# Router logits computed with the tokens as the stationary operand, straight into token rows

## The chip, the cores and the metric

One Trainium2 chip, one of its cores. The metric is the device time of one launch in microseconds (us), lower is better. The kernel before takes 298.62 us, the median of 3 runs (298.42 to 298.67). Its engines are named as the profile names them: PE is TensorE's matmul side, PEld the loading of its stationary operand, ACT is ScalarE, DVE is VectorE, POOL is GpSimd, SP is SyncE.

## The reference

One transformer block over `x` of 8 sequences of 256 tokens, 256 wide: layer norm with adaptive scale and shift, a two-pass attention, a second layer norm, and a mixture of 8 experts with 2 chosen for each token, beside a shared feed-forward part. What the change touches is the router:

```python
h = hidden_states.reshape(-1, H)                                   # 2048 tokens x 256
logits = h.astype(jnp.float32) @ gate_weight.astype(jnp.float32).T # 2048 x 8
scores = jax.nn.softmax(logits, axis=-1)
topk_w, topk_i = _group_limited_topk(scores)
...
g = jnp.einsum('th,nfh->ntf', h, gate_w)
u = jnp.einsum('th,nfh->ntf', h, up_w)
e = jnp.einsum('ntf,nhf->nth', jax.nn.silu(g) * u, down_w)
routed = jnp.einsum('nth,tn->th', e, wmat)
shared = jax.nn.silu(h @ sh_gate_w.T) * (h @ sh_up_w.T) @ sh_down_w.T
```

## The kernel before

There are three stretches. Until about 142 us of the profile, attention of the 8 sequences `b` is interleaved with the router and the shared feed-forward part of earlier sequences; until about 200 us the rest of the shared part (`pe_up(q, j)`, `pe_down(q)`) runs; then 39 tiles of 128 routed rows go through their experts. Every engine works through a list written out by hand (from line 1502 on), in its own order; engines meet only through semaphores, which are waited for with `wait_ge`. An instruction that waits holds up everything behind it on its engine.

A product in full precision is made of three matmuls (`mm3`, line 341): each operand is kept as a rounded part `_hi` and a remainder `_lo`, and lo x hi, hi x lo and hi x hi are added in PSUM. The first operand of `mm3` is the stationary one, which is loaded into the array; the second one is streamed through it.

The router runs in pairs of sequences `p` (512 tokens, 4 blocks of 128). For each sequence `b`: `dve_h2` makes the normalised rows, `pe_h2t` transposes them into a PSUM bank (`post_bank(b)`, bank `HB[1]` except for `b` = 7), `act_h2` copies the rounded part into `h2T_hi`, and `dve_h2_lo` subtracts to get `h2T_lo` (semaphore `h2_lo`). `pe_logits(b)` then takes the 8 columns of router weights `wrt` as stationary operand and streams 256 tokens, for 2 halves `k` of the width: 6 matmuls, and a result of 8 rows x 256 tokens. `act_lg(b)` copies it to SBUF (`lg`), and `pe_logits_t(p)` transposes the four blocks of a pair into token rows, 128 x 8 each, in `LOG` (columns 0 to 31 of `HB[1]`). `dve_select(p, 0)` waits for these (`lt_done`), and two rounds of top-1 follow; then `pe_rank(p)` counts the slots of each expert, `dve_slots` and 8 indirect DMAs of POOL (`pool_scatter`) write the rows to DRAM.

Four orders matter for the steps below. Behind `pe_logits(0)` on PE stands `pe_v(4)` (line 1066), which waits for ACT to have emptied its banks (`act_qk(5, 0)`). Behind `pe_logits(2)` stands `pe_pt(5, True)` (line 1109), which waits for the exponentials of sequence 5 (`act_exp`, line 1137). Behind `pe_logits(3)` stand `pe_s1(7)` and `pe_up(1, 1)`, which waits for a product of DVE (`dve_gate(1, 0)`, line 457). Behind `pe_logits(4)` stands `pe_up(2, 0)`, which waits for `dve_og(1)` (line 471).

Of the kernel before, what the change touches and what calls it, by code (L numbers as in the profile page):

```python
# [28 lines left out]
def adaln_block(nc, x_in, w_qkv, b_cols, w_proj, b_proj, gate_col, cam_w0, cam_w1,  # L29
# [17 lines left out]
    with ExitStack() as ctx:  # L47
        def sb(name, shape, dt=F32):
            return ctx.enter_context(nc.sbuf_tensor(name, shape, dt))
# [4 lines left out]
        def sem(name):  # L54
            return ctx.enter_context(nc.semaphore(name))
# [57 lines left out]
        s_ident_ready = sem("ident_ready")  # L113
        s_lg_copied = sem("lg_copied")
        s_lg_done = sem("lg_done")
        s_lt_done = sem("lt_done")
# [157 lines left out]

        lg = [sb(f"lg{u}", [NE, S]) for u in range(2)]
        sact = [sb(f"sact{u}", [P, S]) for u in range(2)]
# [61 lines left out]
        def parts(t, *idx):  # L338
            return t[0][idx], t[1][idx]
# [190 lines left out]
        def pe_h2t(pe, b):  # L530
            pe.wait_ge(s_h2_ready, b + 1)
            if b == B - 1:
                pe.wait_ge(s_og_ready, 3)
            elif b % 2:
                pe.wait_ge(s_lg_copied, b)
            elif b >= 2:
                pe.wait_ge(s_slots_ready, b // 2)
            for d in range(KD):
                for t in range(TT):
                    last = pe.transpose(post_bank(b)[:, d * S + t * P:d * S + (t + 1) * P],  # L540
                                        h2all[:, b % 4 * TT + t, d * P:(d + 1) * P], ident[:])
            last.then_inc(s_h2t_done, 1)

        def pe_logits(pe, b):
            pe.wait_ge(s_wlo_later, 1)
            pe.wait_ge(s_h2_lo, b + 1)
            for k in range(KD):
                last = mm3(pe, post_bank(b)[0:NE, 0:S], parts(wrt, slice(None), k),
                           parts(h2T, slice(None), k, ring4(b)), k == 0, k == KD - 1)
            last.then_inc(s_lg_done, 1)  # L550

# [6 lines left out]
        def dve_h2_lo(dve, b):  # L558
            dve.wait_ge(s_h2_hi, b + 1)
            dve.tensor_tensor(h2T[1][:, :, ring4(b)], bank(post_bank(b)), h2T[0][:, :, ring4(b)].bitcast(F32),  # L560
                              ALU.subtract).then_inc(s_h2_lo, 1)

        def act_lg(act, b):
            act.wait_ge(s_lg_done, b + 1)
            if b >= 2:
                act.wait_ge(s_lt_done, b // 2)
            act.activation(lg[b % 2][:], post_bank(b)[0:NE, 0:S], ACT.Copy).then_inc(s_lg_copied, 1)


        def pe_logits_t(pe, p):  # L570
            pe.wait_ge(s_lg_copied, 2 * p + 2)
            for j in range(NB):
                last = pe.transpose(LOG[:, j * NE:(j + 1) * NE], lg[j // TT][:, j % TT * P:(j % TT + 1) * P], ident[0:NE, 0:NE])
            last.then_inc(s_lt_done, 1)

# [182 lines left out]
        if True:  # L758
# [742 lines left out]
            with nc.Block() as block:  # L1501
# [149 lines left out]
                def _(act):  # L1651
# [66 lines left out]
                    act_qk(act, 5, 0)  # L1718
                    act_lg(act, 0)
                    act_norm(act, 4)  # L1720
# [8 lines left out]
                    act_norm(act, 5)  # L1729
                    act_lg(act, 1)  # L1730
                    act_exp(act, 4, True)
# [16 lines left out]
                    act_qk(act, 7, 1)  # L1748
                    act_lg(act, 2)
                    act_pt(act, 5, True)  # L1750
# [5 lines left out]
                    act_weights(act, 4)  # L1756
                    act_lg(act, 3)
                    act_exp(act, 7, False)
# [18 lines left out]
                    act_gate(act, 2, 0)  # L1777
                    act_lg(act, 4)
                    act_h2(act, 5)
                    act_hi(act, 2, 0)  # L1780
                    act_gate(act, 2, 1)
                    act_lg(act, 5)
                    act_hi(act, 2, 1)
# [13 lines left out]
                    act_h2(act, 7)  # L1797
                    act_lg(act, 6)
                    act_hi(act, 3, 2)
                    act_lg(act, 7)  # L1800
                    act_route(act, 3)
# [236 lines left out]
                def _(pe):  # L2038
# [55 lines left out]
                    pe_up(pe, 0, 0)  # L2094
                    pe_logits(pe, 0)
                    pe_v(pe, 4)
# [7 lines left out]
                    pe_s2_cam(pe, 4)  # L2104
                    pe_logits(pe, 1)
                    pe_up(pe, 0, 1)
                    pe_pt(pe, 5, False)
                    pe_logits_t(pe, 0)
                    pe_qk(pe, 6)
# [10 lines left out]
                    pe_out(pe, 4)  # L2120
                    pe_logits(pe, 2)
                    pe_pt(pe, 5, True)
# [4 lines left out]
                    pe_pt(pe, 6, False)  # L2127
                    pe_logits(pe, 3)
                    pe_s1(pe, 7)
                    pe_up(pe, 1, 1)  # L2130
                    pe_logits_t(pe, 1)
                    pe_v(pe, 6)
# [14 lines left out]
                    pe_pt(pe, 7, True)  # L2147
                    pe_logits(pe, 4)
                    pe_up(pe, 2, 0)
                    pe_out(pe, 7)  # L2150
                    pe_h2t(pe, 5)
                    pe_up(pe, 2, 1)
                    pe_logits(pe, 5)
                    pe_logits_t(pe, 2)
                    pe_up(pe, 2, 2)
# [9 lines left out]
                    pe_h2t(pe, 7)  # L2165
                    pe_logits(pe, 6)
                    pe_logits(pe, 7)
                    pe_logits_t(pe, 3)
                    pe_down(pe, 3)
# [81 lines left out]
```

## Time and profile before

| what | value |
|---|---|
| median of the runs | 298.62 us |
| the profiled execution's own time | 299.12 us |
| its span (first to last instruction) | 297.3 us |
| PE busy, PEld busy | 259.9 us (87%), 240.3 us (81%) |
| DVE, ACT, POOL busy | 190.1, 161.2, 128.4 us |
| chain that ended last, by engine | PE 77%, DVE 5%, ACT 4%, issue 4% |

The span is the part that the trace covers; 1.8 us of the profiled execution's own time lie around it. The chain that ended last is followed back from the last instruction: a change of PE's time counts where PE stands in it. A line number is one of the kernel before.

### The profile page before, as it was taken

How to read it: one execution, taken by the hardware profiler on the slowest of the kernel's cores; microseconds unless marked ns; L12 is line 12 of the kernel's file. 1: busy time of each engine (PE TensorE's matmuls, PEld its weight loads, DVE VectorE, ACT ScalarE, POOL GpSimd, SP SyncE). 2: the span in 40 equal slices, each digit the busy share in tenths (PEclk: the TensorE clock that was granted, in tenths of full speed). 3: DMA queues.
4: the chain of work that ended last, by engine and by line, in shares of the span. 5: the costliest groups of instructions: out<-in, count | busy, mean ns of one | idle time of the engine just before them, and what ended most of it. 6: DMA issues, size and time to landing. Idle time of an engine off the chain costs nothing.

```text
span 297.3 us, 6191 instructions
## 1 busy us (share of the span) xinstructions
PE 259.9 (87%) x1820; PEld 240.3 (81%) x1820; DVE 190.1 (64%) x579; ACT 161.2 (54%) x429; POOL 128.4 (43%) x146
## 2 busy tenths in 40 slices
PE   1799999899999999999997691999999999999900
PEld 1697698778988999979896581999999999999800
DVE  2667765259987754864897552365546566858894
ACT  2538477877558548474374621345656565555500
POOL 3120406454460287769927572001545444544540
PEclk9999999999999999999999996799999999999975
DMA  7893033450242022321501243043444365584454
GB/s 237 279 341 77 0 84 137 117 171 32 77 110 73 1 92 89 110 89 54 165 0 57 90 163 127 4 125 107 128 142 127 128 210 179 179 245 149 150 193 139
DMA packets 29319, 36.98 MB, mean 124 GB/s; under 512 B 4468, under 2 KB 23903, under 8 KB 29288
## 3 DMA queue, kind: packets, MB, share of 16 engines
q1 hardware_dynamic: 24056, 27.19, 30.7%
q0 software_dynamic: 3408, 8.46, 7.6%
q10 hardware_dynamic: 1824, 0.94, 1.1%
q8 instruction: 16, 0.26, 0.4%
q14 instruction: 15, 0.12, 0.1%
HBM read 24.78 MB, written 12.71 MB: 126 GB/s over the span
## 4 chain that ended last, share of the span: by engine, by line
PE 77%; DVE 5%; ACT 4%; issue 4%; another core or an unknown queue 2%; DMA 2%; POOL 2%; ACTq 1%; POOLq 0%; DVEq 0%
PE bank L343 18%; PE bank L345 17%; PE bank L344 17%; PE bank L1133 3%; PE bank L1370 3%; PE bank L1348 3%; PE bank L1105 2%; PE bank L1125 2%; PE bank L1088 2%; PE bank L1116 2%; PE bank L1097 2%; PE bank L1006 1%; DMA mh<-routed_out 1%; DMA routed_out<-yo_all,dest 1%
## 5 line engine op out<-in xcount | busy, mean ns | idle before, releaser
L1436 POOL DMA_INDIRECT routed_out<-yo_all,dest x39 | 40.1, 1028 | 65.1 <-ACT yo_all L1397 49.2
L343 PE MATMUL bank<-experts_w,h2T_lo 128*128 (+1 forms) x156 | 50.7, 325 | 0.0
L345 PE MATMUL bank<-experts_w,h2T_hi 128*128 (+1 forms) x156 | 47.2, 303 | 0.0
L344 PE MATMUL bank<-experts_w,h2T_hi 128*128 (+1 forms) x156 | 47.0, 301 | 0.0
L701 POOL DMA_INDIRECT routed_in<-h2all,slot_u x32 | 31.6, 988 | 21.2 <-DVE slot_u L687 13.3
L1425 DVE SCALAR_TENSOR_TENSOR wstage<-wstage,wt,bank 128x176 f32<-128x176 f32 x39 | 15.5, 397 | 28.8 <-ACT wstage L1387 28.8
L343 PEld LDWEIGHTS bank<-experts_w,h2T_lo 128*128 128x128 f32 (+1 forms) x156 | 29.6, 190 | 0.5 <-issue 0.5
L344 PEld LDWEIGHTS bank<-experts_w,h2T_hi 128*128 128x128 f32 (+1 forms) x156 | 29.7, 190 | 0.0
L343 PE MATMUL bank<-h2T_hi,wsgu_lo 128*128 128x256 f32 (+1 forms) x96 | 28.3, 295 | 1.5 <-issue 1.5
L345 PEld LDWEIGHTS bank<-experts_w,h2T_hi 128*128 128x128 f32 (+1 forms) x156 | 29.4, 188 | 0.0
L345 PE MATMUL bank<-h2T_hi,wsgu_hi 128*128 128x256 f32 (+1 forms) x96 | 27.4, 285 | 0.5 <-issue 0.5
L344 PE MATMUL bank<-h2T_lo,wsgu_hi 128*128 128x256 f32 (+1 forms) x96 | 27.3, 284 | 0.5 <-issue 0.5
L1387 ACT ACTIVATE wstage<-bank 128x176 f32<-128x176 f32 x39 | 12.4, 317 | 22.2 <-PE bank L345 22.2
L343 PE MATMUL bank<-hT_hi,wqk_lo 128*128 128x256 f32 x64 | 20.2, 316 | 2.0 <-DVE hT_lo L1218 2.0
L1397 ACT ACTIVATE yo_all<-bank 128x256 f32<-128x256 f32 x39 | 15.0, 385 | 11.8 <-PE bank L345 7.5
L343 PE MATMUL bank<-wsd_hi,aT_lo 128*128 128x256 f32 (+1 forms) x48 | 15.0, 313 | 6.5 <-DVE aT_lo L463 6.5
L343 PEld LDWEIGHTS bank<-h2T_hi,wsgu_lo 128*128 128x128 f32 (+1 forms) x96 | 17.6, 184 | 2.0 <-issue 1.7
L344 PE MATMUL bank<-hT_lo,wqk_hi 128*128 128x256 f32 x64 | 19.0, 298 | 0.0
L1142 ACT ACTIVATE exchange<-bank,nm 128x256 f32<-128x256 f32 x32 | 14.8, 472 | 7.8 <-DVE nm L1203 6.1
L345 PE MATMUL bank<-hT_hi,wqk_hi 128*128 128x256 f32 x64 | 19.0, 297 | 0.0
L345 PEld LDWEIGHTS bank<-h2T_hi,wsgu_hi 128*128 128x128 f32 (+1 forms) x96 | 17.6, 184 | 1.2 <-issue 1.2
L344 PEld LDWEIGHTS bank<-h2T_lo,wsgu_hi 128*128 128x128 f32 (+1 forms) x96 | 17.6, 184 | 0.1
(248 smaller groups left out, 761.2 us busy)
## 6 DMA issues: line engine op xcount, KB each, us to landing
h2all<-routed_in SPq DMA_DIRECT2D x39, 130.0 KB, 2.1
wstage<-gu_t SPq DMA_DIRECT2D x8, 352.0 KB
res<-x SPq DMA_DIRECT2D x4, 512.0 KB, 8.9
mx<-modrow SPq DMA_DIRECT2D x8, 256.0 KB, 3.8
mh<-modrow SPq DMA_DIRECT2D x8, 256.0 KB
exchange<-routed_out SPq DMA_DIRECT2D x8, 256.0 KB
wmod_s<-w_mod SPq DMA_DIRECT2D x3, 512.0 KB, 9.7
wstage<-down_t SPq DMA_DIRECT2D x8, 176.0 KB
```

Source lines behind the costliest of these rows:

```text
L343: pe.matmul(out_ap, l[1], r[0], start=start, stop=False)
L344: pe.matmul(out_ap, l[0], r[1], start=False, stop=False)
L345: return pe.matmul(out_ap, l[0], r[0], start=False, stop=stop)
L701: pool.indirect_dma_start(out=routed_in, out_offset=bass.IndirectOffsetOnAxis(slot_u[:, i, j:j + 1], 0), in_=h2all[:, j % (2 * NB), :], in ...
L1133: last = pe.matmul(TR[u][:, t * D:(t + 1) * D], PT[u][:, k, t * P:(t + 1) * P], VV[u][:, k, P:P + D], start=(k == 0), stop=(k == TT - 1))
L1142: last = act.activation(pr[u][:, t, :], Sb[u][:, t * S:(t + 1) * S], ACT.Exp, bias=nm[u][:, i, t:t + 1], accum_out=ls[u][:, i, t:t + 1])
L1348: last = pe.transpose(XTb[r % 2][:, d * P:(d + 1) * P], xt_in[t % 8][:, d * P:(d + 1) * P], ident[:])
L1370: last = pe.transpose(ATb[r % 2][0:FH, j * P:(j + 1) * P], av[r % 2][:, j * FH:(j + 1) * FH], ident[:])
L1387: act.activation(sg[r % 2], EGU[r % 2][:, 0:F], ACT.Silu).then_inc(s_esilu, 1)
L1397: act.activation(yo[t % 6], EDN[r % 2][:, 0:D], ACT.Copy).then_inc(s_ey_ready, 1)
L1425: dve.scalar_tensor_tensor(av[q], sg[q], wt[:, t % 8:t % 8 + 1], EGU[q][:, F:2 * F], ALU.mult, ALU.mult).then_inc(s_ea_ready, 1)
L1436: pool.indirect_dma_start(out=routed_out, out_offset=bass.IndirectOffsetOnAxis(dest[:, t % 16:t % 16 + 1], 0), in_=yo[t % 6], in_offset=No ...
```

## The change

`pe_logits` now works on a pair: for each of its four blocks of 128 tokens and each half of the width, the 128 columns of `h2T` are the stationary operand and the 8 columns of `wrt` are streamed, so that the result lands in `LOG` as token rows. The ACT copies `act_lg`, the buffers `lg`, the transposes `pe_logits_t` and two semaphores go. The new group stands where `pe_logits_t(p)` stood in PE's list, and waits for the remainders of both sequences (`h2_lo` of 2p + 2); `pe_h2t` of an odd sequence waits for `h2_lo` of the sequence before it in place of the copy.

```diff
@@ pe_h2t
             elif b % 2:
-                pe.wait_ge(s_lg_copied, b)
+                pe.wait_ge(s_h2_lo, b)
...
-        def pe_logits(pe, b):
+        def pe_logits(pe, p):
             pe.wait_ge(s_wlo_later, 1)
-            pe.wait_ge(s_h2_lo, b + 1)
-            for k in range(KD):
-                last = mm3(pe, post_bank(b)[0:NE, 0:S], parts(wrt, slice(None), k),
-                           parts(h2T, slice(None), k, ring4(b)), k == 0, k == KD - 1)
-            last.then_inc(s_lg_done, 1)
+            pe.wait_ge(s_h2_lo, 2 * p + 2)
+            for b, u in pair_of(p):
+                for t in range(TT):
+                    j = u * TT + t
+                    at = slice(b % 4 * S + t * P, b % 4 * S + (t + 1) * P)
+                    for k in range(KD):
+                        last = mm3(pe, LOG[:, j * NE:(j + 1) * NE], parts(h2T, slice(None), k, at),
+                                   parts(wrt, slice(None), k), k == 0, k == KD - 1)
+            last.then_inc(s_lt_done, 1)
...
-        def act_lg(act, b):
-            act.wait_ge(s_lg_done, b + 1)
-            if b >= 2:
-                act.wait_ge(s_lt_done, b // 2)
-            act.activation(lg[b % 2][:], post_bank(b)[0:NE, 0:S], ACT.Copy).then_inc(s_lg_copied, 1)
-
-        def pe_logits_t(pe, p):
-            pe.wait_ge(s_lg_copied, 2 * p + 2)
-            for j in range(NB):
-                last = pe.transpose(LOG[:, j * NE:(j + 1) * NE], lg[j // TT][:, j % TT * P:(j % TT + 1) * P], ident[0:NE, 0:NE])
-            last.then_inc(s_lt_done, 1)
...
-                    act_lg(act, 0)
...
                     pe_up(pe, 0, 0)
-                    pe_logits(pe, 0)
                     pe_v(pe, 4)
...
                     pe_s2_cam(pe, 4)
-                    pe_logits(pe, 1)
                     pe_up(pe, 0, 1)
                     pe_pt(pe, 5, False)
-                    pe_logits_t(pe, 0)
+                    pe_logits(pe, 0)
                     pe_qk(pe, 6)
...
                     pe_h2t(pe, 7)
-                    pe_logits(pe, 6)
-                    pe_logits(pe, 7)
-                    pe_logits_t(pe, 3)
+                    pe_logits(pe, 3)
                     pe_down(pe, 3)
```

On PE, between the shared part of sequence 0 and the values of sequence 4, the kernel before had these instructions (`wrt` are the router weights, `wv` the value weights; the first shape is that of the result):

```order
L345 MATMUL bank3<-h2T_hi,wsgu_hi 128x256
L343 MATMUL bank3<-h2T_hi,wrt_lo 8x256 [waits h2_lo,wlo_later]
L344 MATMUL bank3<-h2T_lo,wrt_hi 8x256
L345 MATMUL bank3<-h2T_hi,wrt_hi 8x256
L343 MATMUL bank3<-h2T_hi,wrt_lo 8x256
L344 MATMUL bank3<-h2T_lo,wrt_hi 8x256
L345 MATMUL bank3<-h2T_hi,wrt_hi 8x256
L343 MATMUL bank2<-wv_hi,hT0_lo 128x384 [waits kl,qk_second,qk_first,wlo]
```

They are gone from there: `pe_v(4)` now follows the shared part at once, with the same waits.

On PE, at the end of the router of the last pair, ahead of `pe_down(3)` (`lg` is the ACT copy, `wsd` the shared down weights), the kernel before had:

```order
L344 MATMUL bank3<-h2T_lo,wrt_hi 8x256
L345 MATMUL bank3<-h2T_hi,wrt_hi 8x256
L573 MATMUL bank3<-ident,lg0 128x8 [waits lg_copied]
L573 MATMUL bank3<-ident,lg0 128x8
L573 MATMUL bank3<-ident,lg1 128x8 x2
L343 MATMUL bank0<-wsd_hi,aT1_lo 128x256 [waits wlo_later,a_lo_dve]
```

and the kernel after the change has there (the first of 8 such threes, and what stands ahead of them):

```order
L537 MATMUL bank3<-ident,h2all 128x128 [waits og_ready,h2_ready]
L537 MATMUL bank3<-ident,h2all 128x128 x3
L340 MATMUL bank3<-wrt_hi,h2T_lo 128x8 [waits h2_lo,wlo_later]
L341 MATMUL bank3<-wrt_lo,h2T_hi 128x8
L342 MATMUL bank3<-wrt_hi,h2T_hi 128x8
```

Two groups of 6 matmuls with a result of 8 x 256 and four transposes have become one group of 24 matmuls with a result of 128 x 8, and its only waits stand at its head.

## Rows read from the trace of the kernel before

**Rows 1.** The page, parts 1 and 4: busy time, and the chain's shares.
```profile
PE 259.9 (87%) x1820; PEld 240.3 (81%) x1820; DVE 190.1 (64%) x579; ACT 161.2 (54%) x429; POOL 128.4 (43%) x146
...
PE 77%; DVE 5%; ACT 4%; issue 4%; another core or an unknown queue 2%; DMA 2%; POOL 2%; ACTq 1%; POOLq 0%; DVEq 0%
```

**Rows 2.** Groups of instructions: busy us, mean ns of one | idle before, releaser.
```profile
L343 PE MATMUL bank<-h2T_hi,wrt_lo 128*8 128x256 f32 x16 | 4.9, 307 | 1.2 <-DVE h2T_lo L560 1.1
...
L343 PEld LDWEIGHTS bank<-h2T_hi,wrt_lo 128*8 128x8 f32 x16 | 1.4, 87 | 2.1 <-issue 1.7
...
L343 PEld LDWEIGHTS bank<-h2T_hi,wsgu_lo 128*128 128x128 f32 x64 | 12.1, 189 | 1.9 <-issue 1.7
...
L567 ACT ACTIVATE lg<-bank 8x256 f32<-8x256 f32 x8 | 2.9, 363 | 1.7 <-PE bank L345 1.0 <-issue 0.6
```

**Rows 3.** Timeline, PE: start us, us, engine, line, stationary*shape, streamed shape [idle before].
```profile
6.40 3.56 PE L998 MATMUL bank<-cS,wmod_s 128*128 128x8 f32 x16 [6.40 <-DVE cS L909]
...
15.18 0.41 PE L345 MATMUL bank<-hT_hi,wqk_hi 128*128 128x256 f32 x1
15.39 0.41 PE L343 MATMUL bank<-hT_hi,wqk_lo 128*128 128x256 f32 x1
...
100.47 0.29 PE L597 MATMUL bank<-r_sel,ones 128*128 128x24 bf16 x6
```

**Rows 4.** Timeline, PE and (last row) ACT, 80 to 96 us: pair 0.
```profile
80.28 0.28 PE L343 MATMUL bank<-h2T_hi,wsgu_lo 128*128 128x256 f32 x1
...
81.70 0.28 PE L343 MATMUL bank<-h2T_hi,wrt_lo 128*8 128x256 f32 x1
...
83.11 0.41 PE L343 MATMUL bank<-wv_hi,hT_lo 128*128 128x384 f32 x1 [0.55 <-issue]
...
94.79 0.41 PE L573 MATMUL bank<-ident,lg 8*128 8x8 f32 x4
95.13 0.39 PE L343 MATMUL bank<-hT_hi,wqk_lo 128*128 128x256 f32 x1
...
82.54 0.48 ACT L1183 ACTIVATE KT<-bank,cols 128x256 f32<-128x256 f32 x1
```

**Rows 5.** Timeline, PE, ACT and DVE, 108 to 129 us: pair 1.
```profile
109.13 0.60 PE L1116 MATMUL bank<-ident,exchange 128*128 128x128 f32 x4
...
117.99 0.39 PE L343 MATMUL bank<-h2T_hi,wsgu_lo 128*128 128x256 f32 x1
...
119.62 0.41 PE L573 MATMUL bank<-ident,lg 8*128 8x8 f32 x4
...
128.43 0.66 PE L1116 MATMUL bank<-ident,exchange 128*128 128x128 f32 x4 [0.54 <-ACT exchange L1150]
...
108.45 0.20 ACT L1142 ACTIVATION_READ_ACCUMULATOR exchange<-bank,nm 128x1 f32 x1
...
117.52 0.42 DVE L457 TENSOR_TENSOR aact<-aact,bank 128x256 f32<-128x256 f32 x1
```

**Rows 6.** Timeline, DVE and PE, 137 to 146 us: pair 2.
```profile
137.41 0.69 DVE L471 TENSOR_TENSOR og<-bank,gring 128x512 f32<-128x512 f32 x1 [2.41 <-issue]
...
142.77 0.69 DVE L560 TENSOR_TENSOR h2T_lo<-bank,h2T_hi 128x512 fp32r<-128x512 f32 x1 [0.19 <-ACT h2T_hi L556]
...
138.34 0.28 PE L343 MATMUL bank<-h2T_hi,wsgu_lo 128*128 128x256 f32 x1
...
145.27 0.36 PE L343 MATMUL bank<-h2T_hi,wsgu_lo 128*96 128x256 f32 x1
```

**Rows 7.** Timeline, DVE and PE, 159 to 163 us: pair 3.
```profile
159.03 1.46 DVE L560 TENSOR_TENSOR h2T_lo<-bank,h2T_hi 128x512 fp32r<-128x512 f32 x2 [0.72 <-ACT h2T_hi L556]
...
162.30 0.39 PE L343 MATMUL bank<-wsd_hi,aT_lo 128*128 128x256 f32 x1
```

**Rows 8.** Windows (stretch, length, PE busy, granted clock), and longest waits.
```profile
184.50:190.20 5.70, 5.70 (x26) 0.50 0.07 23
...
ACT sact L435 <- remote: 7.0, 1, 7.0
```

More of the change, by code:

```diff
@@ L113, in adaln_block @@
         s_ident_ready = sem("ident_ready")
-        s_lg_copied = sem("lg_copied")
-        s_lg_done = sem("lg_done")
         s_lt_done = sem("lt_done")
@@ L272, in adaln_block @@
         slot_u = sb("slot_u", [P, 2, NR], U32)
-        lg = [sb(f"lg{u}", [NE, S]) for u in range(2)]
         sact = [sb(f"sact{u}", [P, S]) for u in range(2)]
@@ L1729, in _ @@
                     act_norm(act, 5)
-                    act_lg(act, 1)
                     act_exp(act, 4, True)
@@ L1748, in _ @@
                     act_qk(act, 7, 1)
-                    act_lg(act, 2)
                     act_pt(act, 5, True)
@@ L1756, in _ @@
                     act_weights(act, 4)
-                    act_lg(act, 3)
                     act_exp(act, 7, False)
@@ L1777, in _ @@
                     act_gate(act, 2, 0)
-                    act_lg(act, 4)
                     act_h2(act, 5)
@@ L1781, in _ @@
                     act_gate(act, 2, 1)
-                    act_lg(act, 5)
                     act_hi(act, 2, 1)
@@ L1797, in _ @@
                     act_h2(act, 7)
-                    act_lg(act, 6)
                     act_hi(act, 3, 2)
-                    act_lg(act, 7)
                     act_route(act, 3)
@@ L2120, in _ @@
                     pe_out(pe, 4)
-                    pe_logits(pe, 2)
                     pe_pt(pe, 5, True)
@@ L2127, in _ @@
                     pe_pt(pe, 6, False)
-                    pe_logits(pe, 3)
                     pe_s1(pe, 7)
                     pe_up(pe, 1, 1)
-                    pe_logits_t(pe, 1)
+                    pe_logits(pe, 1)
                     pe_v(pe, 6)
@@ L2147, in _ @@
                     pe_pt(pe, 7, True)
-                    pe_logits(pe, 4)
                     pe_up(pe, 2, 0)
@@ L2152, in _ @@
                     pe_up(pe, 2, 1)
-                    pe_logits(pe, 5)
-                    pe_logits_t(pe, 2)
+                    pe_logits(pe, 2)
                     pe_up(pe, 2, 2)
```

## The prediction

> **What bounds the kernel now.** I read the page's busy times and the shares of the chain first: PE is busy 87% of the span and holds 77% of the chain that ended last [rows 1]. So time added to PE counts, unless PE was going to wait there anyway, and time taken from ACT (54%) counts only where PE waits for it. Then the groups of instructions: the router's product is 48 matmuls, three groups like the one shown, with 8 stationary and 256 streamed columns; the copies are 8, of 363 ns [rows 2]. Then the timeline around each of the four pairs, for what PE waits for there [rows 4 to 7].
>
> **The pace of a matmul.** Durations of PE are latencies that overlap, so the cost is the distance between starts. With 128 stationary and 256 streamed columns it is (81.70 - 80.28) / 12 = 0.118 us [rows 4]; loading only 8 stationary columns makes it no faster, since the 256 streamed ones set it. After the change 128 columns are loaded and 8 streamed, and the load has to set the pace. A load of 8 columns takes 87 ns and one of 128 takes 189 ns [rows 2]: 102 ns for 120 more columns. The one place with this very shape is L998: 16 in 3.56 us, and with the last one's 0.36 taken off, 3.20 / 15 = 0.213 between starts [rows 3]. The clock was at its lower level there: the 256-column matmuls after it start 0.21 apart [rows 3], as they do (5.70 / 26 = 0.219) where the granted clock is 0.50 [rows 8]. At the full clock half of 0.213 is 0.107.
>
> Ends for the new shape: from below 0.048, the bf16 matmuls of the rank (0.29 / 6 [rows 3]), or 0.085, the four transposes with 128 loaded and 8 streamed columns ((95.13 - 94.79) / 4 [rows 4]); from above 0.189, a whole load with nothing beside it. Since loads of this kind already fit under a pace of 0.118, I take the middle of 0.107 and 0.118, 0.112. A pair's 24 matmuls then take 2.69 us. Before, it had 12 x 0.118 = 1.42 for the products and 0.34 for the transposes. So PE gets 0.93 us more work a pair; where PE waited, the old work was partly free, and I go pair by pair.
>
> The Trainium skill (TensorE: Matmul & The Clock Gate, section LDWEIGHTS) prices a load by its columns, at 1.2 GHz: 128 of them make 107 ns, which the halved pace of L998 bears out. The same page, section on what overlaps in packed matmuls, says that a load runs beside a matmul only in another row group; by that each of the 24 would pay the load in full, 0.189, and the sum below would be 11.9 us instead of 4.5. The trace disagrees: loads of 189 ns stand under a pace of 0.118.
>
> **Pair 0.** Taking `pe_logits(0)` (6 x 0.118 = 0.71) from its place gains nothing: `pe_v(4)` behind it starts at 83.11 because ACT empties its bank until 82.54 + 0.48 = 83.02 [rows 4]. Taking `pe_logits(1)` gains 0.70; the transposes and the wait for the copy ahead of them 0.43 (0.34, and 0.09 above the normal distance). Net +2.69 - 1.13 = +1.56.
>
> **Pair 1.** `pe_logits(2)` hid a wait: the transposes behind it, at 109.13, need exponentials that end at 108.65, so they move up by 0.43 at most [rows 5]. `pe_logits(3)` gains nothing: `pe_up(1, 1)` at 117.99 follows the product that DVE ends at 117.94 [rows 5], whatever PE does before. Transposes and wait: 0.44. Net +2.69 - 0.87 = +1.82. Then comes the cover: PE sat idle 0.54 ahead of 128.43 for ACT's normalised scores [rows 5], and being late fills that gap, -0.54. That holds although the selection starts later on DVE, with the scores' reciprocal queued behind it: DVE starts it about 2.9 us later, has some 0.9 of idle time to give back, and is then still ahead of PE. Net +1.28.
>
> **Pair 2.** Taking `pe_logits(4)` moves `pe_up(2, 0)` from 138.34 only to the end of DVE's product at 138.10: -0.2 with the semaphore [rows 6]. The new group needs `h2_lo` of both, which DVE ends at 143.46; 0.05 for the semaphore and 2.69 end it at 146.20, where the next group began at 145.27 [rows 6]: +0.93. Net +0.73. Here ACT's copies did stand in the path, and their going is in this number.
>
> **Pair 3.** Both remainders are ready at 159.03 + 1.46 = 160.49 [rows 7]. Before, PE began on sequence 6 at 159.87, ahead of that; the added wait costs this head start. 160.54 + 2.69 = 163.23 against 162.30 [rows 7]: +0.93. Behind the waiting matmul stand `pe_down(3)`, the rank and the order; ACT's `act_shared(3)`, the slots, the scatters and the tables wait for these, so all of it moves by the same.
>
> ACT loses 8 x 0.36 = 2.9 us [rows 2]; beyond the places named, it lies beside PE and gives nothing. DMAs and queues are not touched. From 164 us on the work is the same and hangs on PE's order, so I cost it at nothing.
>
> **Sum.** 1.56 + 1.28 + 0.73 + 0.93 = 4.50 us on 299.12, 303.6; on the median, which lies 0.5 lower, 303.1. In general it is 96 times the pace less 6.26 us. At 0.107 the time is 302.6, at 0.118 303.7; at 0.085 300.5; at 0.189 310.5. Zero is at 0.065.
>
> **Rival 1, the load costs little (not slower).** If the array takes the next 128 columns in the background as fast as it does for the bf16 rank, the streamed columns set the pace and 8 are almost none. At 0.048 the group of 24 takes 1.15 and the pairs give +0.02, 0, -0.81 and -0.61: -1.4, 297.2. With the latency of one taken off, the rank's pace is 0.024, and the same sum is about -3.5, 295.1. It decides below 0.065. For it: rank and transposes load 128 columns at that pace [rows 3, 4]. Against: these are bf16 or transposes, and loads of the router's kind take 102 ns more for 120 more columns.
>
> The Trainium skill (same page, Back-to-back issue gap) has a rule for this rival: a warm matmul of 1 to 64 streamed columns costs about 60 cycles, an estimate of 0.6 us for a group of 24. Its section on loads speaks against it; L998 sides with the loads.
>
> **Rival 2, the clock falls.** For 2.7 us PE would stream almost nothing, four times, in pair 3 right after an idle stretch. After L998's 3.56 us of the same shape the clock was still at the lower level [rows 3]. A fall cost, the one time it is seen, 26 starts in 5.70 us instead of 26 x 0.118 = 3.07: 2.6 us [rows 8]. One fall gives 305.7, two 308.3, four 313.5. Against it: the clock stayed up through 160 us with several waits of PE of 1 to 2 us, and L998 began on an idle engine, so it doesn't tell whether this shape would hold a clock that is up.
>
> **Rival 3, the long wait at 176 us changes.** ACT waits 7.0 us for a matmul group's semaphore that the trace ascribes to no engine [rows 8]; PE then stands idle and restarts at the lower clock, 6.5 + 2.6 = 9.1 us together. If PE's shifted schedule dissolves it, the time is 294.0; it could also grow by some us. Against: scatters, their semaphores and PE's order all shift alike.
>
> **How the numbers follow.** Forecast (300.5 to 304.5) 0.46; rival 2 0.30; rival 1 0.12; rival 3 0.12, of which 0.07 shorter. The predicted time is 303.1. A measurement of this kernel can tell about 0.2% (0.6 us) from no change. Faster: 0.11 of rival 1 and 0.07 of rival 3, 0.18. Within: 0.04, from paces near 0.065. Slower 0.78. The range goes from 297.0 (half of rival 1 inside) to 310.5 (three falls of the clock, or loads without any overlap); about 0.13 is left below and 0.07 above.
>
> **What would show it.** The starts of the 24 matmuls: 2.6 to 2.8 us a group says the load sets the pace, 0.6 to 1.2 says rival 1. The granted clock in and after the groups tells rival 2. `pe_v(4)` should still begin right after ACT's KT; `pe_up(1, 1)` right after DVE's product; PE's idle time ahead of the scores of sequence 7 should be gone; PE's copy waits ahead of the transposes too. The expert stretch should have its old length, and the long wait of ACT should be there again, some 4.5 us later. Wrong would be a shift of the last router group's end by less than 3 us, or idle time of PE that is new.

## The result, and the profile after

The changed kernel takes 309.32 us (median of 4 runs, 308.26 to 310.76) against 298.52 for the kernel before beside it: 1.0364 of it, 95% interval 1.0329 to 1.0399. It is 10.8 us slower, where 4.5 were forecast, and the time lies inside the range given, at its upper end. The profiled execution took 308.83 us, its span is 307.1, and the mean granted clock 0.935 against 0.963. First the busy times and the chain's shares (page, parts 1 and 4), which answer to [rows 1]:

```profile
PE 271.4 (88%) x1852; PEld 253.8 (83%) x1852; DVE 190.3 (62%) x579; ACT 158.4 (52%) x421; POOL 128.2 (42%) x146
...
PE 78%; ACT 6%; DVE 5%; issue 4%; DMA 2%; another core or an unknown queue 2%; ACTq 1%; POOLq 0%; POOL 0%; DVEq 0%
```

PE is busy 11.5 us longer with 32 instructions more. The timeline of PE shows the group of pair 0 and the product behind it, which answers to [rows 4] (start us, us, engine, line, operands):

```profile
93.08 0.25 PE L340 MATMUL bank<-wrt_hi,h2T_lo 128*128 128x8 f32 x1
...
95.65 0.25 PE L342 MATMUL bank<-wrt_hi,h2T_hi 128*128 128x8 f32 x1
95.77 0.36 PE L340 MATMUL bank<-hT_hi,wqk_lo 128*128 128x256 f32 x1
...
96.40 0.41 PE L341 MATMUL bank<-hT_lo,wqk_hi 128*128 128x256 f32 x1
...
99.39 0.39 PE L340 MATMUL bank<-hT_hi,wqk_lo 128*128 128x256 f32 x1
```

The 24 matmuls take 95.77 - 93.08 = 2.69 us, 0.112 each: the pace assumed. But behind them the matmuls of 256 columns start (99.39 - 96.40) / 14 = 0.214 us apart, where the kernel before has 0.118. The windows say why (stretch, length, then busy us of each engine, granted clock, DMA share, GB/s); they answer to [rows 8]:

```profile
92.00:96.20 4.20, 4.20 (x39) 4.20 (x38) 1.44 (x5) 2.19 (x8) 0.00 (x0) 1.00 0.19 48
96.20:99.60 3.40, 3.40 (x18) 3.40 (x17) 2.84 (x14) 1.25 (x3) 0.00 (x0) 0.50 0.00 0
...
123.50:126.90 3.40, 3.40 (x13) 3.40 (x13) 2.46 (x12) 0.00 (x0) 2.85 (x4) 0.50 0.58 159
...
150.80:154.20 3.40, 3.40 (x18) 3.40 (x18) 1.25 (x10) 0.38 (x1) 2.96 (x4) 0.50 0.23 80
...
167.90:181.50 13.60, 12.80 (x76) 12.41 (x77) 6.03 (x27) 5.28 (x11) 5.94 (x7) 0.50 0.17 59
...
195.20:198.60 3.40, 3.22 (x15) 3.22 (x16) 0.45 (x2) 0.00 (x0) 0.00 (x0) 0.50 0.12 39
```

The clock is at 0.50, 1.2 GHz, four times behind or in a router group, and once more behind the idle stretch at the end. The first fall comes after 4.2 us in which PE shows no idle time at all; for 2.7 of them it had streamed 8 columns a matmul. The expert stretch is as long as before: from the first to the last matmul that reads expert weights (the last two times of each row, first of the kernel before, then of the change; tile experts_w) it is 82.4 and 82.3 us.

```profile
L343 PE MATMUL bank<-experts_w,h2T_lo x156: 277/323/408, 199.8 to 282.2; 128*128 x78, 88*128 x78
L340 PE MATMUL bank<-experts_w,h2T_lo x156: 277/323/407, 209.6 to 291.9; 128*128 x78, 88*128 x78
```

Three rows answer to [rows 4, 5]: ACT's KT and `pe_v(4)`, then DVE's product, `pe_up(1, 1)` and the scores of sequence 7.

```profile
81.68 0.48 ACT L1171 ACTIVATE KT<-bank,cols 128x256 f32<-128x256 f32 x1
82.26 0.41 PE L340 MATMUL bank<-wv_hi,hT_lo 128*128 128x384 f32 x1 [1.25 <-ACT KT L1171]
...
119.14 0.42 DVE L454 TENSOR_TENSOR aact<-aact,bank 128x256 f32<-128x256 f32 x1
119.61 0.39 PE L340 MATMUL bank<-h2T_hi,wsgu_lo 128*128 128x256 f32 x1
...
133.08 0.60 PE L1104 MATMUL bank<-ident,exchange 128*128 128x128 f32 x4
```

Both waits stand where they were forecast, right behind ACT's KT and DVE's product, and the idle time ahead of the scores is gone. Pairs 2 and 3 (timeline, DVE and PE) answer to [rows 6, 7]:

```profile
147.26 0.69 DVE L561 TENSOR_TENSOR h2T_lo<-bank,h2T_hi 128x512 fp32r<-128x512 f32 x1 [0.19 <-ACT h2T_hi L557]
150.77 0.48 PE L340 MATMUL bank<-h2T_hi,wsgu_lo 128*96 128x256 f32 x1
...
166.05 1.46 DVE L561 TENSOR_TENSOR h2T_lo<-bank,h2T_hi 128x512 fp32r<-128x512 f32 x2 [0.72 <-ACT h2T_hi L557]
167.65 0.24 PE L340 MATMUL bank<-wrt_hi,h2T_lo 128*128 128x8 f32 x1 [1.83 <-DVE h2T_lo L561]
172.56 0.56 PE L340 MATMUL bank<-wsd_hi,aT_lo 128*128 128x256 f32 x1
...
195.38 0.58 PE L340 MATMUL bank<-wsd_hi,aT_lo 128*128 128x256 f32 x1 [4.23 <-DVE aT_lo L460]
```

Pair 2: 2.8 us from the end of DVE's remainder to the next group, as forecast. Pair 3: PE waits for both remainders, and the clock falls just after the group has begun, so that it takes 172.56 - 167.65 = 4.9 us, not 2.7. Against [rows 4 to 7] the kernel is late by 0.64 at 95.77, 4.65 at 133.08, 5.50 at 150.77 and 10.26 at 172.56; at 195.38 it is 10.88 [rows 8], and the whole profiled execution 9.71. It had been 13.1 late at 190.62, ahead of PE's idle stretch, where the kernel before was at 177.50. ACT's long wait is there again, but 5.5 us in place of 7.0, PE's idle stretch 4.2 in place of 6.5, and the half clock at the end of it lasts 3.4 us with 3.2 of work in place of 5.7 [rows 8]. At the first expert matmul the kernel is 9.8 late (209.6 against 199.8). So 3.3 us (13.1 to 9.8) of what was lost came back there:

```profile
ACT sact L432 <- remote: 5.5, 1, 5.5
```

### The profile page after: what moved, and what is told of

It reads as the page before. It is cut to its first block, busy times and chain, and to the rows that moved or that the text cites. A ratio compares the mean times of both kernels' runs of the same rounds, so it can differ in the third digit from the quotient of the medians.

```text
span 307.1 us, 6237 instructions
## 1 busy us (share of the span) xinstructions
PE 271.4 (88%) x1852; PEld 253.8 (83%) x1852; DVE 190.3 (62%) x579; ACT 158.4 (52%) x421; POOL 128.2 (42%) x146
## 4 chain that ended last, share of the span: by engine, by line
PE 78%; ACT 6%; DVE 5%; issue 4%; DMA 2%; another core or an unknown queue 2%; ACTq 1%; POOLq 0%; POOL 0%; DVEq 0%
PE bank L340 19%; PE bank L342 18%; PE bank L341 18%; PE bank L1358 3%; PE bank L1336 3%; PE bank L1076 2%; PE bank L1113 2%; PE bank L1121 2%; PE bank L1085 2%; PE bank L1093 2%; PE bank L1104 2%; DMA mh<-routed_out 1%; PE bank L994 1%; DMA routed_out<-yo_all,dest 1%
## 5 line engine op out<-in xcount | busy, mean ns | idle before, releaser
L340 PE MATMUL bank<-h2T_hi,wsgu_lo 128*128 128x256 f32 (+1 forms) x96 | 29.8, 311 | 2.5 <-issue 1.4
L341 PE MATMUL bank<-h2T_lo,wsgu_hi 128*128 128x256 f32 (+1 forms) x96 | 28.3, 295 | 0.0
L342 PE MATMUL bank<-h2T_hi,wsgu_hi 128*128 128x256 f32 (+1 forms) x96 | 28.2, 294 | 0.0
L340 PEld LDWEIGHTS bank<-h2T_hi,wsgu_lo 128*128 128x128 f32 (+1 forms) x96 | 18.6, 194 | 3.1 <-ACT og L474 1.1
L341 PEld LDWEIGHTS bank<-h2T_lo,wsgu_hi 128*128 128x128 f32 (+1 forms) x96 | 18.7, 195 | 0.6 <-issue 0.6
L342 PEld LDWEIGHTS bank<-h2T_hi,wsgu_hi 128*128 128x128 f32 (+1 forms) x96 | 18.6, 194 | 0.0
```

Source lines behind the costliest of these rows:

```text
L340: pe.matmul(out_ap, l[1], r[0], start=start, stop=False)
L341: pe.matmul(out_ap, l[0], r[1], start=False, stop=False)
L342: return pe.matmul(out_ap, l[0], r[0], start=False, stop=stop)
```

## The experiments

One thing has to be known to read the times: the kernel before took 298.5 and 299.3 us on two of the chips and 287.9, 288.1 and 288.5 on three others. On the latter ACT's long wait, PE's idle stretch behind it and its half clock are all missing (below). So each run is set against the kernel before on its own chip, and the clean account is made where that wait is missing.

| kernel | us | before | ratio (95%) |
|---|---|---|---|
| e1 wide streams | 304.87 | 299.28 | 1.0176 (1.0104 to 1.0249) |
| e2 old form, new places | 302.39 | 299.28 | 1.0123 (1.0055 to 1.0191) |
| e3 pair 0 only | 300.18 | 299.28 | 1.0056 (1.0019 to 1.0093) |
| e4 mixed | 316.52 | 299.28 | 1.0589 (1.0522 to 1.0656) |
| e5 filler | 293.41 | 287.85 | 1.0197 (1.0166 to 1.0228) |
| e6 only pair 3 wide | 297.11 | 287.85 | 1.0328 (1.0287 to 1.0369) |
| e7 pair 3 only | 292.46 | 287.85 | 1.0169 (1.0128 to 1.0210) |
| e8 late pads | 299.19 | 287.85 | 1.0415 (1.0365 to 1.0466) |
| e9 the change again | 299.30 | 288.06 | 1.0421 (1.0358 to 1.0484) |
| e10 wide streams again | 291.39 | 288.06 | 1.0136 (1.0086 to 1.0186) |
| e12 pair 0 only, again | 290.30 | 288.06 | 1.0088 (1.0058 to 1.0119) |
| e13 fewer loads, wide | 290.07 | 288.46 | 1.0056 (1.0039 to 1.0073) |
| e14 fewer loads, narrow | 291.75 | 288.46 | 1.0097 (1.0070 to 1.0124) |
| e15 old form, new places, again | 292.65 | 288.46 | 1.0138 (1.0118 to 1.0158) |
| e16 filler again | 293.27 | 288.46 | 1.0164 (1.0141 to 1.0187) |

**Is it the few streamed columns?** e1 and e10 stream 256 columns:

```diff
-                        last = mm3(pe, LOG[:, j * NE:(j + 1) * NE], parts(h2T, slice(None), k, at),
-                                   parts(wrt, slice(None), k), k == 0, k == KD - 1)
+                        last = mm3(pe, HB[1][:, j * NE:j * NE + 32 * NE].rearrange("p (r e) -> p r e", e=NE),
+                                   parts(h2T, slice(None), k, at),
+                                   [wrt[i][:, k:k + 1, :].to_broadcast([P, 32, NE]) for i in range(2)],
+                                   k == 0, k == KD - 1)
```

> The new form with one difference: each of the 96 matmuls streams 256 columns (the 8 router columns repeated 32 times) in place of 8; same 128 loaded columns, same places, same waits. Theory (the clock falls because these groups stream almost nothing): no half-clock stretch at the four groups, pace 0.118 a matmul, group of 24 in 2.8 us, time 303.2 to 304.6 us although 31 times as many columns are streamed. Rival 1 (it is the loads, or the places and waits, that lose the time): the surplus stays and the wider streams add 96 x 0.006 = 0.6, 309.9 us. Rival 2 (the falls happen but are worth little): half-clock stretches gone, time above 307.

Windows of e1 (it runs on a chip where that wait is there): no half clock until 172.8 us, that is none at any of the four groups, but one behind an idle stretch that is new, and the one at the end.

```profile
92.00:172.80 80.80, 74.13 (x570) 69.71 (x568) 51.20 (x180) 38.89 (x98) 48.14 (x50) 1.00 0.22 72
172.90:179.70 6.80, 5.98 (x44) 5.89 (x45) 3.48 (x14) 4.66 (x10) 1.21 (x2) 0.50 0.01 4
```

The new stretch hangs on a wait of ACT for a finished PE group of the shared down product, given to no engine (longest waits of e1); it muddied the time, which is 0.3 us above the range expected.

```profile
ACT og L474 <- remote: 4.7, 1, 4.7
```

> The new form with 256 streamed columns in all four groups. Theory: no half clock anywhere but at the end of the kernel, and no late semaphores: the forecast of 4.5 us plus 0.6 for the wider streams, 4.6 to 5.6 us above before; the rest of the changed kernel's surplus is then the clock. If this chip has the late semaphores: 4 to 8 above, as on the other one.

Here there is no such wait for a semaphore and no half clock from 13 to 276 us, and 32 times the streamed columns make the kernel 7.9 us faster than the change (291.39 against 299.30, same chip), with the same loads, places and waits in the program. It came in at +3.9 us (interval 2.5 to 5.4), a little under what was expected.

**The change on such a chip**, and its kernel before, for the account:

> The changed kernel as it is. On the chip of the last runs the kernel before took 287.85 us and neither it nor its variants had the late semaphores of PE, the idle stretch of 6.5 us and the half clock behind it. Theory: there the changed kernel has nothing to give back at the end, so the four falls of the clock cost in full: 11.5 to 13 us above before (on the first chip 10.8). If this chip has the late semaphores: 10 to 11 above.

> The kernel before, for its trace on this chip. Theory: where its time is near 288 us there is no PE semaphore over 1 us late behind 174 us, no idle stretch of PE over 2 us at 178 us and no half clock before the end; where it is near 299 us all three are there.

It is 12.1 us slower (interval 10.3 to 13.9), in the middle of what was expected. The kernel before took 288.37 us in that run, with no wait given to "remote" at all. Timelines of PE at six marks (the scores of sequence 5; then the instruction behind pair 0's group, the transposes of the scores of sequence 7 for pair 1, the instructions behind the groups of pairs 2 and 3; and one of the expert stretch), first of the kernel before, then the change, then the wide one:

```profile
74.72 0.81 PE L1088 MATMUL bank<-KT,QT 128*128 128x256 f32 x3
95.04 0.39 PE L343 MATMUL bank<-hT_hi,wqk_lo 128*128 128x256 f32 x1
128.34 0.44 PE L1116 MATMUL bank<-ident,exchange 128*128 128x128 f32 x2 [0.54 <-ACT exchange L1150]
145.17 0.36 PE L343 MATMUL bank<-h2T_hi,wsgu_lo 128*96 128x256 f32 x1
162.18 0.39 PE L343 MATMUL bank<-wsd_hi,aT_lo 128*128 128x256 f32 x1
239.98 0.33 PE L343 MATMUL bank<-experts_w,h2T_lo 128*128 x1
```

```profile
72.70 0.81 PE L1076 MATMUL bank<-KT,QT 128*128 128x256 f32 x3
94.46 0.36 PE L340 MATMUL bank<-hT_hi,wqk_lo 128*128 128x256 f32 x1
131.83 0.49 PE L1104 MATMUL bank<-ident,exchange 128*128 128x128 f32 x3
149.45 0.34 PE L340 MATMUL bank<-h2T_hi,wsgu_lo 128*96 128x256 f32 x1
170.60 0.56 PE L340 MATMUL bank<-wsd_hi,aT_lo 128*128 128x256 f32 x1
250.17 0.33 PE L340 MATMUL bank<-experts_w,h2T_lo 128*128 x1
```

```profile
72.65 0.81 PE L1078 MATMUL bank<-KT,QT 128*128 128x256 f32 x3
94.51 0.28 PE L340 MATMUL bank<-hT_hi,wqk_lo 128*128 128x256 f32 x1
128.69 0.49 PE L1106 MATMUL bank<-ident,exchange 128*128 128x128 f32 x3
146.40 0.28 PE L340 MATMUL bank<-h2T_hi,wsgu_lo 128*96 128x256 f32 x1
164.43 0.28 PE L340 MATMUL bank<-wsd_hi,aT_lo 128*128 128x256 f32 x1
242.10 0.33 PE L340 MATMUL bank<-experts_w,h2T_lo 128*128 x1
```

Runs reach the first mark at times that differ by up to 2 us whatever the kernel, so each column below is the distance from that mark, less the same of the kernel before:

| late by, us | forecast | wide (e10) | change (e9) | of it clock |
|---|---|---|---|---|
| behind pair 0 | 1.56 | 1.54 | 1.44 | 0 |
| at the scores, pair 1 | 2.84 | 2.42 | 5.51 | 3.1 |
| behind pair 2 | 3.57 | 3.30 | 6.30 | 3.0 |
| behind pair 3 | 4.50 | 4.32 | 10.44 | 6.1 |
| in the expert stretch | 4.50 | 4.19 | 12.21 | 8.0 |

The last column is the one before it less the wide one. Up to 128 us two falls have cost 3.1, 1.5 each; the third stands behind pair 2 and is in the row of pair 3, with the half pace of pair 3's group.

**One fall at a time.** In e3 and e12 pair 0 alone has the new form, in e7 pair 3 alone; in e6 all have it, with wide streams in pair 3 (the second line is cut short; the rest is as in e1):

```diff
+                        if p == 3:
+                            last = mm3(pe, HB[1][:, j * NE:j * NE + 32 * NE]...
```

> The new form for pair 0 alone; pairs 1 to 3 as before. Theory, with the shifts read from the trace after the change: group +1.5, half clock behind it +1.45, 0.5 of it given back by 109 us: +2.4, 300.9 us (300.2 to 301.6), with one half-clock stretch right behind the group. Prediction's price for a fall (2.6): 302.7. Rival (the loss is nearly all pair 3's, whose half-clock stretch is four times as long; pair 0 costs the pace only): 299.5 to 300.0.

> The new form for pair 0 alone. Theory: one half-clock stretch of 3.4 us behind the group, step +1.5, stretch +1.45, of which 0.5 is absorbed: 2.4 to 3.0 us above before. Rival (a fall is absorbed by later waits for other engines): 1.5 above.

> The new form for pair 3 alone; pairs 0 to 2 as before. Theory: half clock at this group as in the changed kernel, and nowhere earlier; the step +0.93, half pace of the group and of what follows up to +4.4, given back up to 3.3 by the shorter idle stretch at the end: 299.5 to 303 us. Rival (pair 3 costs only its step): 299.4 us with no half clock at the group.

> The changed kernel, with 256 streamed columns for the group of pair 3 alone; pairs 0 to 2 stream 8 as in the change. Theory: the half-clock stretches behind pairs 0 to 2 stay, 3.4 us each, the one of 13.65 us at pair 3 goes; group of pair 3 in 2.8 us instead of 4.9. 4.4 us gained there, of which the idle stretch at the end, full length again (6.5 instead of 4.5 us, 5.7 us of work at half clock instead of 3.4), takes back 3.3: 306.5 to 309 us. Rival (the wait of 2.1 us ahead of the group drops the clock of pair 3, not its few columns): half clock there as before, 309.5 us.

e3 came in lower than expected (300.18; it lies on a chip with late semaphores, and its interval, 0.6 to 2.8 us, doesn't exclude the 2.4), e12 as expected, +2.5. Windows of e12, e7 and e6: one fall, one fall, and three falls, of which the row shown is the stretch behind the third.

```profile
95.10:98.40 3.30, 3.30 (x17) 3.30 (x17) 2.58 (x13) 1.29 (x3) 0.00 (x0) 0.50 0.00 0
98.50:275.90 177.40, 170.16 (x1312) 161.79 (x1311) 118.11 (x381) 98.72 (x278) 96.05 (x97) 1.00 0.40 126
```

```profile
161.10:167.80 6.70, 6.70 (x32) 6.44 (x31) 3.44 (x20) 0.23 (x1) 5.00 (x6) 0.50 0.28 99
```

```profile
154.40:284.00 129.60, 122.50 (x973) 119.16 (x972) 87.92 (x279) 70.72 (x204) 58.22 (x57) 1.00 0.44 140
```

e7 is +4.9 us (3.7 to 6.1), a little above the 1 to 4.5 expected: pair 3 costs the most, as its group itself is slowed. e6 is +9.4 (8.3 to 10.6). Its wait ahead of pair 3 is that of the change (its group starts at 167.65 us behind 1.83 idle, in both), and the clock stayed up, so with 24 wide matmuls behind it the wait alone did not drop it. The time that I gave for e6 was reckoned on the first chip; its rival, half clock at pair 3, is refuted for this form. Against the wide kernel's +3.9 on another chip three falls cost 5.5, 1.8 each; by the starts of the first expert matmul in the two traces it is 1.6 each.

**The places, and the number of loads.** e2 and e15 put the old form in the new places; e13 loads the rounded tokens once for both parts of the weights, 16 matmuls for a pair in place of 24, still wide, and DVE adds the two results; e14 is the same with 16 or 8 streamed columns (its loop, the rest cut):

```diff
+                    for k, part in ((0, 0), (0, 1), (1, 1), (1, 0)):
+                        if part:
+                            pe.matmul(HB[1][:, cols], h2T[1][:, k, at], wrt2[:, k, 0, :], start=False, stop=False)
+                            continue
+                        last = pe.matmul(both, h2T[0][:, k, at], wrt2[:, k, :, :], start=k == 0, stop=k == 1)
```

> The old form (8 stationary, 256 streamed, ACT copies, transposes) put where the new group stands, so that placement alone changes: both products of a pair in one go, after both remainders; both copies after both products. Theory: no half-clock stretch at the groups, and the cover lost (product of sequences 0, 2, 3 and 6 no longer beside waits) plus about 1 us a pair for PE's wait for two copies, +4 to +6, 302.5 to 304.5 us. Rival (the new places are what drops the clock, whatever form stands there): half-clock stretches at the groups, 307 to 310 us.

> The old form in the new places, copies and transposes kept. The first time it was 1.0123 of before, on a chip with late semaphores; its shift up to the end of pair 3 was 4.4 us. Theory: 4 to 4.6 us above before where semaphores are on time, no half clock.

> The wide form of the new group with fewer loads: while the rounded tokens are loaded, rounded weights and remainders are streamed together (2 x 8 columns, each repeated 16 times: 256), the token remainders stream 128; 16 matmuls for each pair in place of 24. DVE adds the two halves (two small operations more at the head of the selection). Theory (the number of loads sets the group: 64 x 0.115 in place of 96 x 0.118, and the covers lost are the rest): 3.9 us less than the wide form that took 1.0136 of before, so 0 to 1 us above before where semaphores are on time. Rival (the surplus of the wide form is the lost cover of the new places alone): 3 to 4 us above.

> The same 16 matmuls a pair, but streaming only their 16 or 8 columns. The group is 1.8 us long in place of 2.7. Theory for the pace: as the wide one, 0.112 a matmul. Theory for the clock: four falls again would make it 7 us above before (1.45 each behind pairs 0 to 2, about 3 at pair 3); none would make it 0 to 0.5 above. Open which; the trace tells how short a group without columns must be in these places.

The old form in the new places costs +4.0 us (3.4 to 4.6, e15) and has no half clock until the end of the kernel. That is as much as the wide new form, but not for the places alone: PE now waits 0.7 us for two copies ahead of the transposes of pair 0. e2, the same kernel on the chip with the long wait, came to 302.39, just under its range; it has no half clock at its groups either, but one of 3.4 us from about 170.3 us on, 6 us behind pair 3's transposes. e13 is +1.6 us, a little above what was expected; up to the end of pair 3's group it is 2.9 us ahead of the wide form for 32 loads fewer, 0.09 each, and that although the clock fell inside this group. So the number of 128-column loads is the main part of what is left without the clock. Windows of e13 and of e14, at pairs 0 and 3, and between those of e13 the first matmul of its group at pair 3 (timeline):

```profile
93.50:97.00 3.50, 3.50 (x31) 3.50 (x31) 2.85 (x14) 1.29 (x3) 0.00 (x0) 1.00 0.00 0
...
159.04 0.35 PE L558 MATMUL bank<-wrt,h2T_hi 128*128 128x256 f32 x1 [1.83 <-DVE h2T_lo L570]
...
160.20:163.60 3.40, 3.40 (x18) 3.40 (x18) 1.99 (x11) 0.00 (x1) 2.48 (x4) 0.50 0.22 78
```

```profile
95.60:99.00 3.40, 3.40 (x31) 3.40 (x30) 2.97 (x14) 1.29 (x3) 0.00 (x0) 1.00 0.00 0
...
162.10:172.30 10.20, 9.51 (x60) 9.12 (x61) 5.71 (x29) 4.88 (x10) 5.22 (x6) 0.50 0.22 79
```

Narrow groups of 1.8 us did not drop the clock behind pairs 0 to 2. At pair 3, where PE has just waited 1.83 us, both fell, the wide one for 3.4 us and the narrow one for 10.2. So few columns alone do not account for pair 3: in e13 the clock fell 1.2 us after the group had begun, behind matmuls of 128 and 256 columns only, and in the change it fell 0.25 us after (1.0 in e9), when the third narrow one had just begun. The wait seems to belong to the cause there. But e6 and e10, with the same wait and 24 wide matmuls, kept the clock. Nor does the length of a wait tell: in e2 the clock fell 1.4 us behind an idle stretch of 1.98 us with wide matmuls on both sides, and in e3 one of 2.93 us at the same place did not drop it. What makes the clock fall at pair 3 is open. In time e14 is +2.8 us (2.0 to 3.6), between the two cases expected: one fall of the four.

**Mixed with wide matmuls.** e4 puts three of the new matmuls at a time between those of the product that follows:

```diff
-                    pe_logits(pe, 0)
-                    pe_qk(pe, 6)
+                    mixed = Mixed(pe, pe_logits_in_threes(pe, 0), 3)
+                    pe_qk(mixed, 6)
```

> The new form with its 24 matmuls of a pair not in one go: three of them at a time between the matmuls that stood behind the group (24 of the queries and keys of sequence 6, 8 of the values of sequence 6, 24 of the shared part, 16 of the shared down product), so that streams of 256 or 384 columns stand between them. Theory: the same loads and columns, but no half-clock stretch at pairs 0 and 2; at pairs 1 and 3, where 3 light ones stand for each 1 or 2 wide ones, open. 303 to 305 us with none, 305 to 307 with one or two. Rival (placement of waits or loads): 309, since all work is the same. Later selection (by up to 2.8 us) costs nothing or is part of the upper end.

The diff shows pair 0; the other three pairs are mixed in the same way. This failed on both counts, time and clock. At pairs 0 and 1 the clock stayed up, but at pairs 2 and 3 it fell for some 10.2 us each (windows of e4), although in the mixture three of every six matmuls at pair 2, and two of every five at pair 3, streamed 256 columns:

```profile
149.90:160.00 10.10, 10.10 (x50) 10.10 (x49) 4.05 (x20) 2.27 (x7) 2.96 (x5) 0.50 0.04 13
173.80:183.90 10.10, 8.98 (x51) 8.60 (x51) 4.23 (x22) 3.81 (x8) 3.49 (x4) 0.50 0.18 63
```

The mixture is a longer stretch of half the columns, and PE waits ahead of both: 1.4 us at pair 2 and 3.4 at pair 3, where the change waits 1.8. So that thinning the group out is enough behind a wait is refuted; what it does without one only pairs 0 and 1 show. Nor is all of e4's loss the clock. Its mean granted clock is 0.937, the change's 0.935, yet its ratio is 1.0589 against 1.0364. The mixture also changes PE's waits: each group now stands behind those of the product that it is mixed with, and at 99.39 us, with the clock up, PE stands idle 1.65 us for DVE's product, a wait that e10 does not have.

**The long wait.** e5 and e16 fill PE's idle stretch of the kernel before, e8 moves the small transfers of SyncE behind all scatters:

```diff
+                    pe_fill(pe, 44)
                     pe_down(pe, 5)
```

> The kernel before, plus 44 matmuls of 256 streamed columns into an unused bank, put on TensorE where it stands idle for 6.5 us from 178 us on (ahead of the shared down product of sequence 5). They take 44 x 0.118 = 5.2 us of that idle time and their results are not used. Theory (the half clock behind the idle stretch is a price of its own, 26 starts in 5.70 us instead of 3.07): no half clock at 184 us, 2.6 us faster than before, 0.991 of it (295.9 us); added work makes the kernel faster. Rival 1 (work in the gap doesn't hold the clock, or the semaphores that end the gap come later by as much): same as before or up to 1 us slower. Rival 2 (the gap closes only because PE waits, and 44 are too many where the gap is short): +0 to +2 us.

> The kernel before with 44 unused matmuls ahead of the shared down product of sequence 5. On the chip without late semaphores it cost 5.5 us, its own length. Theory, if this chip has them (before near 299): 2.6 us faster than before, since PE doesn't restart at half clock; if not: 5.5 us slower again.

> The kernel before, with the 8 small transfers of rows of zeros that SyncE issues from 174 us on put behind the end of all scatters. It asks what holds the semaphores that PE's finished matmuls should give at 175 to 178 us (they come at 182.7). Theory A (the traffic of SyncE's transfers with the scatters holds them): PE's idle stretch of 6.5 us and the half clock behind it shrink or go, and the first tile waits for the late transfers instead (they need some 3 us behind the last scatter): 290 to 296 us. Theory B (the scatters of GpSimd alone hold them): idle stretch as before, 298.5 to 300 us.

All three met chips without the idle stretch, where they cost their own length (44 x 0.117 = 5.1 us by the starts in the trace of e16; +5.6 and +4.8 by the medians) or, in e8, put the transfers in the path (+11.3): PE waits 8.9 us for the rows of the first tile, and a half clock of 10.2 us lies there. They say nothing on what they were made for: what holds the semaphores, and what the half clock behind them is worth, stays open.

## Why the prediction was wrong

**Right.** The pace: 0.112 us in all groups at the full clock, so that loads of 128 columns set it; rival 1 is refuted. By the rule of the Trainium skill (TensorE: Matmul & The Clock Gate, section on what overlaps in packed matmuls) each load would stand alone; 24 matmuls in 2.69 us with loads of 0.19 disagree. What each pair gains and loses: the forecast of 4.50 was 4.19 in the expert stretch of e10, whose groups take 2.76 us in place of 2.69, some 0.3 more in all. For the narrow pace that makes 3.9 (an estimate), so the sum was 0.6 too high. Most of it lies at pair 1: 1.28 forecast, 0.88 measured with the wider streams. `pe_v(4)`, `pe_up(1, 1)`, the gap ahead of the scores, both remainders at pairs 2 and 3, and the unchanged expert stretch came as said.

**Wrong.** The step that failed is the sum of 4.50 us, which the paragraph on how the numbers follow takes as its likeliest case: it counts the granted clock at nothing, and the clock's fall got a chance of 0.30. It fell at all four groups, in each trace of the change, and e10 against e9 shows that this is 8.0 us of 12.2. The mechanism was on record, as rival 2; that the time lies inside the range is owed to the room that the range left for it. What I had against it, that the clock stayed up through several waits of 1 to 2 us, was the wrong comparison: those waits stood between stretches of 256-column matmuls. What I had for it, L998 streaming the same shape for 3.56 us with the clock still low behind it [rows 3], pointed the right way. I set it aside since that engine had been idle before.

**Rival 2's sizes.** Its price, 2.6 us a fall from one stretch [rows 8], was too high for pairs 0 to 2 (1.5 each) and too low for pair 3 (8.0 less three times 1.5 to 1.6, some 3.3), where the group itself ran at half pace. Four falls would by it have been 10.4 us; they were 8.0.

**Rival 3.** The long wait was in the way of the count on the first chip: it came late and shorter, and the half clock behind it took 3.4 us where it had taken 5.7 of work. The traces show this; the times alone do not, for the change cost 10.8 there (interval 9.8 to 11.9) and 12.1 (10.3 to 13.9) where no such wait exists. The 294.0 us of that rival mixed a property of the chip with one of the kernel.

No version beats the kernel before. The best of the new form is e13, 1.0056 of it; without a fall at pair 3 it would be nearer, which wasn't tried.

## What to carry to other kernels

Before making the wide operand the stationary one, count two things: loads of 128 columns cost 0.112 us each however little is streamed, and a train of 24 of them with few streamed columns dropped the clock although the engine shows as busy all the time. Then all that follows pays, 1.5 us a time here and about twice that where a wait of PE stands ahead and the group itself is slowed. If the form is wanted, streaming copies of the small operand into unused columns costs almost nothing and kept the clock up in groups of 24 (7.9 us faster here), and fewer loads help more than thinning them out; but behind a wait of PE the clock fell even in a wide group of 16. Read the granted clock in windows right behind such groups, and compare kernels on one chip.

## What was not expected of the hardware

- The clock fell on a PE with no idle time: 4.20 us busy of 4.20 up to 96.20 us. The Trainium skill (TensorE: Matmul & The Clock Gate, section on why this matters for your kernels) asks to avoid idle gaps between bursts; here there was none, and the measurement decides.
- On two chips ACT waited up to 7 us, at 175 to 190 us, for the semaphore of a PE group whose matmuls had long ended in the trace; on three others it did not. The kernel before takes 298.5 us on one and 288.1 on the other, 10.5 apart; its two traces agree to 0.1 us up to the end of pair 3's group (162.30 and 162.18) and are 11.0 apart at the first expert matmul (199.78 and 188.79). That it is a late semaphore is read from the waits; what holds it is not shown. In e1 one more wait of this kind, 4.7 us, stands at 169 us, so this can move with the schedule.
- Repeating a streamed operand with a stride of zero (8 columns 32 times) ran at the normal pace of 256 columns: group of 24 in 94.51 - 91.75 = 2.76 us in e10.
